# A four-layer block on one core: two scan groups moved one unit later, and the latent attention with a ring of six banks and values by tokens

## What is computed

```python
# 1: gated recurrence
z = sigmoid(x @ Wz + bz);  h_t = (1 - z_t) * h_(t-1) + z_t * (x @ Wh + bh)_t      # per sequence
# 2: six layers of local attention (16 heads of 64, window 32) and a gated feed-forward
# 3: latent attention
q = rope((x @ Wqa @ Wqb).reshape(b, s, 16, 8));  kv = (x @ Wkva @ Wkvb).reshape(b, s, 4, 8, 2)
k, v = rope(kv[..., 0]), kv[..., 1]                # 4 key/value heads, each for 4 query heads
w = softmax(causal(q @ k.T * 8 ** -0.5));  out = (w @ v) @ Wout + bout
# 4: mixture of 8 experts, the best 2 of each token
```

## Time and profile before

| what | us |
|---|---|
| median of 3 runs (lowest, highest) | 2133.55 (2131.57, 2133.88) |
| the profiled execution, its span | 2131.08, 2129.2 |
| the first block, up to the first turns of queries and keys | 0 to 73.8 |
| six layers, eight sequences each | 31 to 1792 |
| latent attention and router | 1792 to 2025 |
| tables and experts | 2025 to 2129.2 |

### The profile page before, as it was taken

How to read it: one execution, slowest core, us unless ns; L and a number is a source line. 1 busy time by engine, 2 the same in 40 slices (tenths; PEclk the granted TensorE clock), 3 DMA queues, 4 the chain that set the end, 5 groups by cost and what they waited for, 6 DMA issues and landing times. The chain is left out here.

```text
span 2129.2 us, 64823 instructions
## 1 busy us (share of the span) xinstructions
PE 1999.3 (94%) x21611; PEld 1399.3 (66%) x21611; DVE 1534.3 (72%) x3516; ACT 1692.5 (79%) x4279; POOL 1455.5 (68%) x1662
## 2 busy tenths in 40 slices
PE   6799999999999999999999999999999997988696
PEld 3466666666666666666666666666666665655486
DVE  5777777777777777777777777777777764788654
ACT  3589898989898989898989898989898985655355
POOL 4687878787878787878787878777777762244343
PEclk8899999999999999999999999999999999999888
DMA  3232223222233222323222322223544242000023
GB/s 96 49 72 55 57 71 82 64 57 54 59 84 75 56 58 53 90 63 68 52 59 69 84 62 59 52 60 83 119 98 103 51 105 84 2 12 11 15 61 107
DMA packets 191396, 138.95 MB, mean 65 GB/s; under 512 B 47758, under 2 KB 183636, under 8 KB 191172
## 3 DMA queue, kind: packets, MB, share of 16 engines
q1 hardware_dynamic: 189028, 133.09, 26.4%
q0 software_dynamic: 2272, 4.72, 0.7%
HBM read 28.36 MB, written 14.96 MB: 20 GB/s over the span
## 5 line engine op out<-in xcount | busy, mean ns | idle before, releaser
L975 ACT ACTIVATE pr<-bank,mx 128x64 f32<-128x64 f32 x1536 | 336.9, 348 | 0.3 <-DVE mx L1078 0.2
L1160 POOL TENSOR_TENSOR qr<-t 128x512 f32<-128x512 f32 x192 | 245.8, 1280 | 130.4 <-DVE t L1058 130.3
L1057 DVE TENSOR_TENSOR t<-bank,rot_t 128x512 f32<-128x512 f32 x384 | 262.8, 684 | 99.7 <-PE bank L813 93.5
L1148 POOL TENSOR_TENSOR qr<-qr,rn 128x512 f32<-128x512 f32 x192 | 201.0, 1047 | 173.3 <-DVE rn L1029 173.3
L1058 DVE TENSOR_TENSOR t<-bank,rot_t 128x512 f32<-128x512 f32 x384 | 261.1, 680 | 0.0
L1163 POOL TENSOR_TENSOR kr<-t 128x512 f32<-128x512 f32 x192 | 245.7, 1280 | 1.0 <-DVE t L1058 1.0
L1166 POOL TENSOR_TENSOR sqh<-sq 128x512 f32<-128x512 f32 x192 | 245.6, 1279 | 0.0
L937 ACT ACTIVATE sq<-bank 128x512 f32<-128x512 f32 x192 | 114.3, 596 | 156.1 <-DVE t L1058 151.6
L983 ACT ACTIVATE kBD<-bank 64x512 f32<-64x512 f32 x384 | 229.0, 596 | 3.1 <-PE bank L530 0.8
L813 PE MATMUL bank<-wqkv,xs 128*128 128x512 f32 x384 | 208.1, 624 | 9.3 <-issue 6.4
L864 PE MATMUL bank<-kBD,qT 128*32 128x128 f32 x6144 | 207.5, 276 | 0.4 <-ACT bank L918 0.3
(11 more groups left out here) (252 smaller groups left out, 4332.6 us busy)
## 6 DMA issues: line engine op xcount, KB each, us to landing
vBD<-vS SPq DMA_DIRECT2D x1152, 64.0 KB, 2.0
vBD<-vS SPq DMA_DIRECT2D x576, 32.0 KB, 1.8
wqkv<-in_L_ffn_Wqkv_dram SPq DMA_DIRECT2D x12, 768.0 KB, 6.6
rows<-const SPq DMA_DIRECT2D x4, 2244.0 KB, 11.2
wo<-in_L_ffn_Wo_dram SPq DMA_DIRECT2D x12, 256.0 KB, 2.9
t<-rows SPq DMA_DIRECT2D x39, 66.0 KB, 1.8
vBD<-in_L_ffn_W_dram SPq DMA_DIRECT2D x1, 2048.0 KB, 8.5
vBD<-in_L_ffn_W_dram SPq DMA_DIRECT2D x8, 256.0 KB, 7.1
```

The lines of the kernel that those rows point to most:

```text
L975: ins = act.activation(pr[:, slot % 2, hd, :], bank[5][:, hd * 64:(hd + 1) * 64], ACT.Exp, bias=mx[:, slot % 2, hd:hd + 1])
L1057: dve.tensor_tensor(t1[:, m], src, tab[:, 0, :].unsqueeze(1).broadcast_to([P, HH, DH]), ALU.mult)
L1148: pool.tensor_tensor(x, x, rn[:, slot, half * HH:(half + 1) * HH].unsqueeze(2).broadcast_to([P, HH, DH]), ALU.mult).then_inc(norm.sem, 1)
L1160: pool.tensor_tensor(qr[:, slot].rearrange("p (h d) -> p h d", d=DH), t1[:, 0], t2[:, 0], ALU.add).then_inc(q_add.sem, 1)
```

## The change

In the first block: the gate semaphore counts each of the two gate products, so ACT's sigmoid waits for the first and DVE's sum for the second; gates of groups 0 and 1 move ahead of the next group's `wide_out`; the first turn of the second norm moves ahead of group 1's `wide_turn`; groups 2 and 3 go one unit later in part (`wide_turn` 2 behind unit 1, the turn of second norm 2 into unit 4), while group 3's gates stay in unit 0 and its scan moves from unit 2 to unit 1. Group 3 gets buffers of its own in `kr` and `qr`.

In the latent attention: scores and turns share six banks in a ring; turns of rows 0 and 1 take the two banks that the scores don't use, rows 2 and 3 the banks of score rows 0 and 1; scores of rows 2 and 3 wait for the copies of the previous unit's turns 0 and 1. ACT copies two rows in m = 0 and 2 and three in m = 1. The values product has the turned weights (`cpT`, 128x128) as its stationary operand and 8 values and a one (`cvo`, 9 columns) as the moving one, so its output has tokens on the partitions, and bank 1 holds 9 numbers for each head. The reciprocal is over 32 sums, the multiply spreads it, two new transposes turn the result back (into bank 1) and ACT keeps it as `conT` for the output product. `cvn`, `cvj`, `conesb` and POOL's work on them go.

```diff
+        cvo = sq[:, :, :].rearrange("p h d -> p (h d)")[:, 0:NT * KVH * (QD + 1)].rearrange("p (k r d) -> p k r d", k=NT, r=KVH)
         late = attT[:, :, :].rearrange("p c k -> p (c k)")
-        con, crd = late[:, 0:SEQ], late[:, SEQ:2 * SEQ]
+        con, conT = late[:, 0:SEQ].rearrange("p (t h d) -> p t h d", t=NT, d=QD), late[:, SEQ:2 * SEQ]
+        crd = late[:, 2 * SEQ:2 * SEQ + NT * QH].rearrange("p (t h) -> p t h", t=NT)
+        outs = bank[1][:, 0:NT * QH * (QD + 1)].rearrange("p (t h d) -> p t h d", t=NT, d=QD + 1)
...
-            for x, y in zip((zs, za, zb, hs), pair):
+        kr_slot = [kr[:, k].rearrange("p h d -> p (h d)") for k in range(UPB)]
+        for group in ((*halves_of(t1), *halves_of(t2)), [qr[:, k, :] for k in range(UPB)], (*halves_of(pr), *halves_of(ob)),
+                      (kr_slot[2], kr_slot[3], qr[:, 2, :], qr[:, 3, :])):
+            for x, y in zip((zs, za, zb, hs), group):
                 x.append(y)
...
+        RING = (4, 5, 6, 7, 2, 3)
+        COPY_ACT = ((0, 2), (0, 1, 2), (0, 2))
+        COPY_DVE = tuple(tuple(r for r in range(KVH) if r not in x) for x in COPY_ACT)
+
+        def score_bank(m, r):
+            return bank[RING[(2 * m + r) % len(RING)]]
+
+        def turn_bank(m, r):
+
+            return bank[RING[(2 * m + KVH + r) % len(RING)]] if r < 2 else score_bank(m, r - 2)
+
+        def turned(a, m, r):
+
+            x, who = (c_pta, COPY_ACT) if r in COPY_ACT[m] else (c_ptd, COPY_DVE)
+            return x, sum(map(len, who)) * a + sum(map(len, who[:m])) + who[m].index(r)
+
+        def wait_turned(eng, a, m, r):
+            x, n = turned(a, m, r)
+            eng.wait_ge(x.sem, x.after(n))
 
...
-                mm = pe.matmul(zh_bank[g][m][:, :], wzh[:, m, :], xn1[g], start=True, stop=True)
-            mm.then_inc(zh_done.sem, 1)
+                pe.matmul(zh_bank[g][m][:, :], wzh[:, m, :], xn1[g], start=True, stop=True).then_inc(zh_done.sem, 1)
 
         def gates_act(act, g):
-            act.wait_ge(zh_done.sem, zh_done.after(g))
-            if g == 3:
-                act.wait_ge(gru_scan.sem, gru_scan.after(2))
+            act.wait_ge(zh_done.sem, zh_done.after(g, 1))
...
             dve.wait_ge(z_sig.sem, z_sig.after(g, 1))
+            dve.wait_ge(zh_done.sem, zh_done.after(g))
...
@@ -663,10 +682,10 @@
             wide_back(pe, 0, 2)
             wide_turn(pe, 0)
             wide_back(pe, 0, 3)
+            wide_back(pe, 1, 0)
             wide_turn(pe, 1)
             gates_pe(pe, 2)
             source_pe(pe, 2)
-            wide_back(pe, 1, 0)
 
         def weave_pe(pe, i, j):
...
@@ -674,25 +693,25 @@
                 return
             if j == 0:
                 wide_back(pe, 1, 1)
+                gates_pe(pe, 3)
+            if j == 1:
+                source_pe(pe, 3)
                 wide_turn(pe, 2)
-                gates_pe(pe, 3)
-                source_pe(pe, 3)
             if j == 2:
-                wide_back(pe, 1, 2)
                 wide_turn(pe, 3)
 
         def gru_act(act):
             act.wait_ge(ld_gru.sem, 16 * 4)
             wide_out(act, 0, 0)
+            gates_act(act, 0)
             wide_out(act, 0, 1)
-            gates_act(act, 0)
+            gates_act(act, 1)
             wide_out(act, 0, 2)
-            gates_act(act, 1)
             keep_act(act, 0)
             wide_out(act, 0, 3)
+            wide_out(act, 1, 0)
             keep_act(act, 1)
             gates_act(act, 2)
-            wide_out(act, 1, 0)
 
         def weave_act(act, i, j):
...
@@ -700,10 +719,10 @@
                 return
             if j == 0:
                 wide_out(act, 1, 1)
+                gates_act(act, 3)
+            if j == 1:
                 keep_act(act, 2)
-                gates_act(act, 3)
             if j == 2:
-                wide_out(act, 1, 2)
                 keep_act(act, 3)
 
...
@@ -717,10 +736,10 @@
             dve.wait_ge(ld_gru.sem, 16 * 4)
             scan_dve(dve, 0)
             wide_normalise(dve, 0, 3)
+            wide_moments(dve, 1, 0)
             scan_dve(dve, 1)
-            wide_moments(dve, 1, 0)
+            wide_normalise(dve, 1, 0)
             wide_moments(dve, 1, 1)
-            wide_normalise(dve, 1, 0)
             wide_normalise(dve, 1, 1)
 
         def weave_dve(dve, i, j):
...
@@ -730,11 +749,11 @@
             if j == 0:
                 scan_dve(dve, 2)
             if j == 1:
+                scan_dve(dve, 3)
+            if j == 2:
                 wide_moments(dve, 1, 2)
-            if j == 2:
+            if j == 3:
                 wide_normalise(dve, 1, 2)
-                scan_dve(dve, 3)
-            if j == 3:
                 wide_moments(dve, 1, 3)
             if j == UPB:
                 wide_normalise(dve, 1, 3)
...
@@ -793,6 +812,7 @@
                     pe.wait_ge(gru_res.sem, gru_res.after(NGR - 1))
                     pe.wait_ge(gru_b.sem, gru_b.after(NGR - 1))
                     pe.wait_ge(z_sig.sem, z_sig.after(NGR - 1))
+                    wide_back(pe, 1, 2)
                     pe.matmul(bank[5][:, :], ident, cst("rot"), start=True, stop=True).then_inc(s_set.sem, 1)
                 if isinstance(i, int) and (i, j) == (1, 0):
...
@@ -920,6 +940,7 @@
 
             for i, j, live, has, unit in units(act):
                 if isinstance(i, int) and (i, j) == (0, UPB):
+                    wide_out(act, 1, 2)
...
+                    if r >= 2 and n:
+                        wait_turned(pe, *divmod(n - 1, NQ), r - 2)
+                    pe.matmul(score_bank(m, r)[:, :], cq[32 * r:32 * r + 32, ap * SEQ + t * P:ap * SEQ + (t + 1) * P],
                               ckm[32 * r:32 * r + 32, ap * GRP + j0:ap * GRP + j0 + nh, 0:nk * P], start=True, stop=False,
                               skip_group_check=True)
...
+                        wait_turned(pe, *divmod(n - 1, NQ), r + 2)
                     for q in range(4):
-                        mm = pe.transpose(bank[2 + r % 2][:, q * P:(q + 1) * P], cp[:, r, q * P:(q + 1) * P], ident)
+                        mm = pe.transpose(turn_bank(m, r)[:, q * P:(q + 1) * P], cp[:, r, q * P:(q + 1) * P], ident)
                     mm.then_inc(c_pt.sem, 1)
 
             def values(a, m):
                 t, j0, nh, nk = QUADS[m]
-                n = NQ * a + m
-                pe.wait_ge(c_pta.sem, c_pta.after(2 * n + 1))
-                pe.wait_ge(c_ptd.sem, c_ptd.after(2 * n + 1))
+                for r in range(KVH):
+                    wait_turned(pe, a, m, r)
                 if m == 0:
-                    pe.wait_ge(c_cv.sem, c_cv.after(a))
-                    pe.wait_ge(c_nrm.sem, c_nrm.after(a - 1))
+                    pe.wait_ge(cv_ev.sem, cv_ev.after(a))
+                    if a:
+                        pe.wait_ge(c_keep.sem, c_keep.after(a - 1))
                 for x in range(4):
                     j, kb = j0 + x // nk, x % nk
-                    for o, ones in ((0, False), (SEQ, True)):
-                        for r in range(KVH):
-                            mm = pe.matmul(bank[1][32 * r:32 * r + 32, o + t * P:o + (t + 1) * P],
-                                           conesb[:, j, :] if ones else cvj[:, kb, r, j, :], cpT[r][:, x * P:(x + 1) * P],
-                                           start=(m == 0 and x == 0 and not ones), stop=(x == 3), skip_group_check=True)
+                    for r in range(KVH):
+                        mm = pe.matmul(outs[:, t, r * GRP + j, :], cpT[r][:, x * P:(x + 1) * P], cvo[:, kb, r, :],
+                                       start=(m == 0 and x == 0 and r == 0), stop=(kb == nk - 1), skip_group_check=True)
                 mm.then_inc(c_o.sem, 1)
 
             pe.wait_ge(cast_done.sem, 2)
             pe.wait_ge(f_res.sem, f_res.after(NI - 1))
-            pe.wait_ge(c_one.sem, 2)
+            pe.wait_ge(c_one.sem, 1)
             pe.wait_ge(ld_late.sem, 16 * (BLANKS + 1))
             for s, par, live in pairs():
...
@@ -1536,6 +1555,11 @@
                             mm.then_inc(c_pq.sem, 1)
                     if live(1):
                         turns(a, m, s - 3 if live(3) else None)
+                    if m == 0 and live(2):
+                        pe.wait_ge(c_nrm.sem, c_nrm.after(c))
+                        for t in range(NT):
...
-                        act.activation(cpT[r], bank[2][:, :], ACT.Copy).then_inc(c_pta.sem, 1)
-
+                    if m == 1 and live(2):
+                        act.wait_ge(c_turn.sem, c_turn.after(s - 2))
+                        act.activation(conT, bank[1][:, 0:SEQ], ACT.Copy).then_inc(c_keep.sem, 1)
...
-                            act.wait_ge(c_cv.sem, c_cv.after(a - 1))
-                            act.activation(cvn[:, :, :, :].rearrange("p t r d -> p (t r d)"),
-                                           bank[0][:, SEQ:SEQ + NT * KVH * QD], ACT.Copy).then_inc(cv_ev.sem, 1)
-                        if m:
-                            keep_turned(0)
-                        keep_turned(2)
```

(10 more changed lines are left out.)

88 lines of the change are left out of this document (34 added, 54 removed).

## The result

The changed kernel took 2190.51 us (median of 4 runs, 2182.25 to 2193.15) against 2132.86 us for the kernel before (median of 4 runs beside it, 2131.57 to 2133.88): ratio 1.0259, 95% interval 1.0232 to 1.0286. The forecast was 2136.5 us with a range of 2127 to 2147; it is wrong by 54 us. The profiled run of after took 2193.15 us, the longest of its four, and its span is 2191.3, so 62.1 us more than the span before.

A forecast was written before the change was run, and what follows sets the result against it. TensorE, busy for 94% of the span, was taken as the bound, with DVE and POOL setting the first block's end. Latent attention +12 and first block -9 gave +3 on 2133.55, so 2136.5 us, range 2127 to 2147.

The forecast's parts named there:

- Values block: Latent attention: 32 instructions with loads 0.112 us apart take 3.6 us, +1.72 each, 24 blocks, +41 us of TensorE work.
- The rival that moving columns set the price: Latent attention: the values block vanishes from TensorE, exps bound the units, 24.2 us instead of 27.07; 2101 us, chance 0.08.
- The issue floor of 25 ns: Values block: published count for 1 to 64 moving columns, would make a block 0.8 us; set against the measured 0.112 us.
- Ring and context's turn: Latent attention: turns without copy waits save 1.57, 1.5 and 1.9 us a unit; turning the context back adds 0.95 per sequence.
- The latent sum at the high level: Latent attention: steady periods 28.2 us against 27.07, +1.15 each; all parts together +12 us, bounds +8 and +20.
- the last sequence: End of the latent attention: +2.6 us, as less other work stands between.
- First block: First 77 us: units start sooner, key and query turns at 64 to 65.5 instead of 73.76; -9 us, bounds -5 and -12.
- scores falling apart: Latent attention, m = 0: DVE's late copy makes the second score pair run by itself; +9 in all, 2145 us, chance 0.18.
- half a first block: First block: low clock or slow DVE pieces put the turns at 69, gain -4; total +8, 2141.5 us, chance 0.10.
- both bounds low: Values block 3.4 us and not 3.6, first block -12; total -5, 2129 us, chance 0.15.
- The tail: Behind the last sequence: short reciprocal saves 1.5 on DVE, but the router's product queues behind the context's turn; -0.5 us.

The follow-up runs named there:

- kernel with 64 columns: Changed kernel with the values' moving operand widened from 9 to 64 columns by zeros, same products and loads: 2137.7 us, ratio 1.0023.
- 32 columns: Changed kernel with the values' moving operand widened from 9 to 32 columns by zeros: 2177.69 us, ratio 1.0218.
- One narrow block: Changed kernel with 64 moving columns in two of a sequence's three values blocks, 9 in that of m = 2: 2150.46 us, ratio 1.0077.
- two to a period: Changed kernel with 9 moving columns in the values blocks of m = 1 and m = 0, 64 in that of m = 2: 2180.2 us, ratio 1.0223.

## Why the prediction was wrong, step by step

**The step that failed** is one that the sum never wrote down: every term of the latent part was priced at the high level of the clock, because the earlier trace rows shows it there; that it would stay there is given no reason, and a fall of the clock in this part is in no rival. The change itself took the high level away. Of the 62.1 us between the two spans, the parts are -11.6 up to the first scores, +69.9 in the latent attention and +3.8 behind it, at a lower clock (0.79 for 0.85); that the clock is the cause of the 3.8 was not tried. The kernel with 64 columns splits the 69.9: its stage takes 227.9 us, so +17.9 is TensorE's own work and waits at a clock of 0.98, and +52.0 is the clock. The rule "half of the time at the low level is lost" gives somewhat more: 134 us at the low level against 9 with 64 columns ((1 - 0.98) / 0.5 of 227.9), half of the difference is some 62. Of the 10 us between, 5.7 are waits that the slow TensorE fills: it is idle for 8.3 us of the stage with 64 columns and for 2.6 with 9. The rest was not taken apart.

The Trainium skill ("TensorE: Matmul & The Clock Gate", section on HAM oscillation) has that rule, throttled time by one minus the clock's share, and names gaps in which the engine waits for a DMA as what brings the level down. The rule's size is near the rows. Its cause is not this case's: the windows above show TensorE busy in 6.80 of 6.80 us up to and through the drops.

**Values block:** 0.109 us a load was right. 32 instructions took 3.5 us to the next start where the clock was high (3.6 forecast), and 6.83 from start to end where it was low throughout. The rival that moving columns set the price fell for fp32; with bf16 weights they count: 0.025 us apart with 9, and (1.06 - 0.22) / 15 = 0.056 with 128. The Trainium skill (same page, section on weight-path perf modes) says that the quick weight load is had by types other than FP32 alone; the runs agree on which is quicker, 0.109 us apart in fp32 and 0.025 in bf16; that is a factor of four, where its table has about two. The issue floor of 25 ns, which the prediction set against the load's price, is by the Trainium skill (same page, section on the back-to-back issue gap) part of a gap that leaves the weight load out, so it was never a price of this block.

**Ring and context's turn:** right at the high level, as the kernel with 64 columns shows: 28.38 us a steady period against 28.2, the wait 0.63 against 0.6, the exps next in line. In the changed kernel itself the later periods took 33.6 to 36.9 us (1892.13 to 1925.71, 1925.71 to 1962.61), and the context's turn had no wait in the stage: TensorE came late.

**The latent sum at the high level:** +17.9 for a forecast of +12, inside its upper bound of 20, though at a clock of 0.98. Steady periods were +1.0 to +1.3 (forecast 1.15); the first three +3.4, +2.8 and +2.2 (2.1, 2.1, 1.6), the first of them with 6.8 us at the low level; the last sequence +4.5 (2.6), with a block of 5.75 us, start to end, at the low level.

**First block:** right in mechanism, small by 2. Unit 0's projection came at 29.52 and not at 31: of the 2 us of the earlier sigmoid, which the forecast counted as lost again, 1.8 were kept. Unit 1's came at 35.90 (38 to 40 forecast), DVE reached unit 3 at 50.94 (53), the norms at 58.14 (60.5), the turns at 62.45 (64 to 65.5). DVE's norm still took 3.01 us, as in the poorer bound; TensorE's granted clock over the first 80 us was 0.87 after 0.77, as in the better one. Alone it is worth 8.5 us at the end, 9 forecast.

**Rivals:** scores falling apart, half a first block, and both bounds low did not decide; none was the one that came. The tail, forecast at -0.5, was 126.6 us with 64 columns and 126.5 before.

With the clock held up, as in the kernel with 64 columns, the time is 2137.7 us, near the forecast of 2136.5. In part that is luck: between the spans its first scores come 11.7 us sooner where the forecast had 9, and its latent attention takes 17.9 more where it had 12.

## What to carry to other kernels

Before swapping a product's operands for fewer instructions, ask for both prices: that of the load (0.109 us for 128 fp32 columns here, whatever moves) and that of the clock, since TensorE, with three blocks of such loads for 9 moving columns to each sequence, lost half its speed for half of a stage. A price read at the high level holds only as long as the work that kept it there stays; when a block is replaced, give the low level a case of its own in the forecast, with its price (here 52 us, where the forecast had +3 for the sum of everything else). Where such a block can't be avoided, filling the moving operand up with zeros was free here: a block took 3.52 us with 64 columns (how far to fill has to be tried: 32 columns did little, 64 nearly all); and a change of several parts is worth trying part by part, since here two sound ones (-8.5 and -13.5 us) were hidden by a third.

## What was not expected of the hardware

- The granted clock fell to 1.2 GHz with TensorE busy in 277 of 280 us: 48% of the stage with 9 moving columns, (1 - 0.81) / 0.5 = 38% of 266 us with 32, 4% of 228 us with 64, the loads being the same.
- One narrow block (3.6 us at the high level) to a period of 30.7 us brought one low stretch each time, mostly of 6.8 us; with two to a period, 12 stretches went with 16 blocks.
- 128-column loads of bf16 weights with 9 moving columns follow each other at 0.025 us, those of fp32 at 0.109, and an fp32 product is two instructions where one of bf16 is one. Shorter is not quicker by itself: blocks of 0.55 us gave 2119 us, and those filled up to 128 columns, 1.06 us long, 2107 us.
